# Routed experts of the first layer: lots of 256 rows followed by lots of 128 rows

## The reference

```python
logits = relu(xf @ Wr1 + br1) @ Wr2 + br2          # xf: [8192, 128]
tg, ti = top_k(softmax(logits), 2)                 # two experts of eight
tg = softmax(tg / 2)
out = silu(xf @ Ws1 + bs1) @ Ws2 + bs2             # shared expert
for e in range(8):
    h = silu(xf @ We1[e] + be1[e]) @ We2[e] + be2[e]
    out = out + sum(tg * (ti == e), -1)[:, None] * h
```

## Time and profile before

| What | Value |
|---|---|
| median of three runs | 1275.22 us (1275.15 to 1275.36) |
| span of the profiled execution, first to last instruction | 1271.2 us |
| PE busy | 1153.3 us, 91% of the span |
| DVE busy | 905.4 us, 71% |
| POOL busy | 746.5 us, 59% |
| ACT busy | 674.7 us, 53% |
| first row of `slot_rows` in TensorE | 487.7 us |
| first matmul of the lead | 768.4 us |

### The profile page before, as it was taken

How to read it: one execution, slowest core, us unless ns; L and a number is a source line. 1 busy time by engine, 2 the same in 40 slices (tenths; PEclk the granted TensorE clock), 3 DMA queues, 4 the chain that set the end, 5 groups by cost and what they waited for, 6 DMA issues and landing times. The chain is left out here.

```text
span 1271.2 us, 27145 instructions
## 1 busy us (share of the span) xinstructions
PE 1153.3 (91%) x9434; PEld 829.7 (65%) x9434; DVE 905.4 (71%) x2795; ACT 674.7 (53%) x1088; POOL 746.5 (59%) x908
## 2 busy tenths in 40 slices
PE   3954999999999997999999998999869899889994
PEld 2642555555555546999999896777647677667773
DVE  8986888888888854666666663888765478874442
ACT  4931877777777773444444343555432255553341
POOL 3204788888888752555555552433337657737886
PEclk9975999999999998999999999999889999999997
DMA  9904000000000011222222223212337412255543
GB/s 328 349 1 180 23 27 27 25 25 23 28 28 27 25 32 44 69 72 69 67 73 67 67 63 106 67 53 65 116 106 245 140 41 61 87 193 93 76 54 31
DMA packets 96816, 104.04 MB, mean 82 GB/s; under 512 B 12812, under 2 KB 84300, under 8 KB 96588
## 3 DMA queue, kind: packets, MB, share of 16 engines
q1 hardware_dynamic: 75792, 75.10, 19.1%
q0 software_dynamic: 19968, 26.63, 8.9%
q10 hardware_dynamic: 956, 0.98, 0.2%
HBM read 55.52 MB, written 47.15 MB: 81 GB/s over the span
## 5 line engine op out<-in xcount | busy, mean ns | idle before, releaser
L829 ACT ACTIVATE probs<-ps 128x1024 f32<-128x1024 f32 x256 | 255.1, 1025 | 76.7 <-PE ps L739 76.7
L1148 POOL DMA_INDIRECT y<-slot_y,where x144 | 150.9, 1048 | 144.8 <-DVE slot_y L1129 121.3
L1037 POOL DMA_INDIRECT slots<-rowbuf,slots x192 | 194.3, 1012 | 67.4 <-issue 42.5
L1216 ACT ACTIVATE slot_h<-ps,own 128x256 f32<-128x256 f32 x288 | 120.3, 470 | 152.7 <-PE ps L1180 151.0
L1180 PE MATMUL ps<-slot_x,own 128*128 128x256 f32 x576 | 139.6, 386 | 4.2 <-DVE slot_x L1118 3.5
L1192 PEld LDWEIGHTS ps<-own,slot_h 128*128 128x128 f32 x1152 | 139.7, 192 | 4.0 <-ACT slot_h L1216 0.4
L1192 PE MATMUL ps<-own,slot_h 128*128 128x128 f32 x1152 | 140.2, 275 | 0.0
L755 PE MATMUL ps<-probs,vext 128*32 128x256 f32 x2048 | 137.4, 386 | 0.0
L1697 ACT ACTIVATE h<-ps,packs 128x512 f32<-128x512 f32 x128 | 85.5, 685 | 86.0 <-PE ps L1525 83.5
L1525 PE MATMUL ps<-xT,packs 128*128 128x512 f32 x256 | 119.7, 605 | 10.7 <-ACT h L1697 10.7
L1180 PEld LDWEIGHTS ps<-slot_x,own 128*128 128x128 f32 x576 | 104.6, 192 | 20.6 <-DVE slot_x L1118 9.1
(11 more groups left out here) (301 smaller groups left out, 2291.6 us busy)
## 6 DMA issues: line engine op xcount, KB each, us to landing
toeplitz<-conv_kernel SPq DMA_DIRECT2D x16, 1024.0 KB, 7.0
slots<-blank SPq DMA_DIRECT2D x26, 528.0 KB, 7.2
slot_rows<-slots SPq DMA_DIRECT2D x72, 132.0 KB, 2.1
routed<-y SPq DMA_DIRECT2D x32, 256.0 KB, 3.1
packs<-in_experts SPq DMA_DIRECT2D x1, 4624.0 KB, 14.2
packs<-in_experts SPq DMA_DIRECT2D x8, 578.0 KB, 6.7
xT<-slots SPq DMA_DIRECT2D x16, 264.0 KB, 2.7
stream<-in_x SPq DMA_DIRECT2D x8, 512.0 KB, 8.1
```

What stands on the lines that cost most here:

```text
L829: act.activation(probs[:, p % 4, :, :, :].rearrange("p j k t -> p j (k t)"), ps[:, 2 * (p % 2):2 * (p % 2) + 2, :], ACT.Exp, scale=DK ** - ...
L1037: return pool.indirect_dma_start(m["slot_dram"][layer], bass.IndirectOffsetOnAxis(ap=where, axis=0), m["rowbuf"][:, tile, :], None)
L1148: pool.indirect_dma_start(m["y_dram"][layer], bass.IndirectOffsetOnAxis(ap=where[:, j, h:h + 1], axis=0), y[:, j, h, :], None).then_inc(se ...
L1216: ins = act.activation(hidden[:, j % 2, k, :], ps[:, 2 * (j % 2) + k // 2, (k % 2) * LOT:(k % 2) * LOT + LOT], act_func, bias=own[:, j, P_ ...
```

## The change

The slots of the first layer are rounded up to 128 rows for each expert instead of 256. An expert with n groups of 128 rows gets n // 2 full lots and, where n is odd, one half lot. The first `WHOLE` = 60 lots are full; `HALF_LOTS` = 15 half lots follow, in which full lots beyond 60 are done as two halves. That makes 75 steps instead of 72, with 17280 rows instead of 18432. The 60 full lots are four written out and 14 rounds of the loop instead of 17. The 15 half lots are written out behind the loop in every engine, with the same buffers, order and waits. In a half lot each operation on rows has half its columns or half its count: one transpose, eight matmuls of 128 columns, eight instead of sixteen in `make_out`, one scatter. The copy of the expert's weights and the operations of lines 1098 to 1107 stay, one for each lot. `place_two` gets more instructions, all on VectorE, and the DRAM array of slots is one chunk shorter, so that there are 25 fills with blank rows instead of 26. The second layer isn't changed.

```diff
-LOTS = (2 * TOKENS // LOT + E, TOKENS // LOT)
+WHOLE = 2 * TOKENS // LOT - E // 2
+HALF_LOTS = 2 * (2 * TOKENS // LOT - WHOLE) + E - 1
+STEPS = WHOLE + HALF_LOTS
...
-    for i in range(count, count + max(lag for _, lag in steps)):
+    for i in range(count, count + more + max(lag for _, lag in steps)):
         for step, lag in steps:
             if i - lag < count:
                 step(i - lag, (i - lag) % buffers)
+            elif i - lag < count + more:
+                step(i - lag, (i - lag) % buffers, True)
...
-                c.link(ts(tmp, size, 1.0 / LOT, 0.5 - 0.5 / LOT, ALU.mult, ALU.add))
-                c.link(ts(tmp, tmp, 1.5 * 2.0 ** 23, None, ALU.add))
-                c.link(ts(tmp, tmp, -1.5 * 2.0 ** 23, None, ALU.add))
-                c.link(dve.tensor_tensor_scan(end, ones[:, 0:E], tmp, 0.0, ALU.mult, ALU.add))
-                c.link(tt(start, end, tmp, ALU.subtract))
-                c.link(stt(place[:, :, :], start.unsqueeze(1).broadcast_to([P, TILES, E]),
-                           float(LOT), place[:, :, :], ALU.mult, ALU.add))
+                c.link(ts(tmp, size, 1.0 / P, 0.5 - 0.5 / P, ALU.mult, ALU.add))
+                c.link(ts(tmp, tmp, MAGIC, None, ALU.add))
+                c.link(ts(tmp, tmp, -MAGIC, None, ALU.add))
+                c.link(ts(pairs, tmp, 0.5, -0.25, ALU.mult, ALU.add))
+                c.link(ts(pairs, pairs, MAGIC, None, ALU.add))
+                c.link(ts(pairs, pairs, -MAGIC, None, ALU.add))
+                c.did(dve.tensor_tensor_scan(end, ones[:, 0:E], pairs, 0.0, ALU.mult, ALU.add))
+                c.link(stt(odd, pairs, -2.0, tmp, ALU.mult, ALU.add))
+                c.did(tt(start, end, pairs, ALU.subtract))
+                c.did(ts(far, end, end[:, E - 1:E], -float(LOT), ALU.subtract, ALU.mult))
+                c.link(dve.tensor_tensor_scan(odd_end, ones[:, 0:E], odd, 0.0, ALU.mult, ALU.add))
+                c.did(ts(start, start, float(LOT), None, ALU.mult))
+                c.did(ts(pairs, pairs, float(LOT), None, ALU.mult))
+                c.link(tt(odd, odd_end, odd, ALU.subtract))
+                c.did(stt(far, odd, float(P), far, ALU.mult, ALU.add))
+                c.link(tt(z[:, :, :], place[:, :, :], wide_e(pairs), ALU.is_ge))
+                c.did(tt(place[:, :, :], place[:, :, :], wide_e(start), ALU.add))
+                c.link(tt(z[:, :, :], z[:, :, :], wide_e(far), ALU.mult))
+                c.link(tt(place[:, :, :], place[:, :, :], z[:, :, :], ALU.add))
...
+                c.did(stt(odd_end, end[:, E - 1:E].broadcast_to([P, E]), 2.0, odd_end, ALU.mult, ALU.add))
...
+                c.link(tt(passed[:, :, :],
+                          cst[:, C_HALF:C_HALF + HALF_LOTS].unsqueeze(2).broadcast_to([P, HALF_LOTS, E]),
+                          odd_end.unsqueeze(1).broadcast_to([P, HALF_LOTS, E]), ALU.is_ge))
+                c.did(dve.tensor_reduce(v[4][:, 0:HALF_LOTS], passed[:, :, :], AX.X, ALU.add))
+                c.link(ts(v[1][:, 0:HALF_LOTS], late, float(E), -float(E), ALU.is_ge, ALU.mult))
+                c.link(tt(late, late, v[4][:, 0:HALF_LOTS], ALU.add))
+                c.link(tt(late, late, v[1][:, 0:HALF_LOTS], ALU.add))
...
+            for i in range(HALF_LOTS):
+                j = i % UNROLL
+                sp.wait_ge(sem["downed"], WHOLE + i + 1)
+                sp.wait_ge(sem["weight_ready"], WHOLE + i + 1)
+                sp.dma_start(rows[:, j, 0, :], half_slots[:, i, :]).then_inc(sem[f"rows{j}"], 16)
...
-                for h in range(HALVES):
+                for h in range(halves(half)):
                     pool.indirect_dma_start(
```

## The result

| | before | after |
|---|---|---|
| median time, beside each other | 1275.29 us (1275.15 to 1275.84) | 1268.45 us (1266.56 to 1269.58) |
| ratio | | 0.9942 (0.9928 to 0.9956) |
| the same two kernels a second time, median | 1274.56 us (1270.95 to 1278.77) | 1269.23 us (1266.17 to 1273.87) |
| ratio | | 0.9960 (0.9944 to 0.9976) |

The change makes the kernel faster by 5 to 7 us, 0.4 to 0.6%. I had forecast no change, 1274.0 us, in a range from 1269.0, which the first median lies under and the second, 1269.23, just inside.

The account below looks back on a forecast made before the run. The prediction took TensorE to bound the lots, with VectorE not far behind and bounding half lots from below. Its sum was 1275.2 - 4.7 (lots) + 3.7 (first stage) = 1274.2, forecast as 1274.0 us, range 1269 to 1279.5.

Parts of the forecast that it names:

- First stage, cost 3.7 us (2.4 to 4.5): Start of the kernel: added table work on VectorE delays the first DMA of `attention` by 3.7 us, bounds 2.4 and 4.5.
- my 4.7: First stage: VectorE's added operations for placing and table, less those removed, take 4.7 us more.
- my 0.9: End of the first stage: 0.9 us of VectorE's added work is hidden, since the barrier waits for the table's last store.
- I count from the turn of lot 60 ..., after which the two kernels part: Lots: the kernels differ only from 714.95 us on; 53.5 us to the lead before the change, earlier full lots unchanged.
- TensorE their bound: Full lots: TensorE, busy 272.4 of 276.9 us, sets their pace at some 3.7 us a lot; VectorE needs 3.0.
- Half lots, 2.6 us a step, saving 4.7 us: Last 15 lots: a step between VectorE's 2.5 and the scatter's 2.76 us; lead after 46.7 instead of 51.4 us.
- The pause: Near lot 60: a wait of 2.79 us at 716.08, 2.1 too long, left in both kernels as a full lot's scatter.
- the rival that it goes: Near lot 60: the long wait isn't repeated, 2.1 us go, 1271.9 us; chance 0.30 together with the lower bounds.
- TensorE at 1.9: Rival for the half lots: TensorE bounds them at 1.9 us a step, 1266.3 us in all; chance 0.05.
- a clock that falls throughout the half lots: Rival: idle TensorE drops to 1.2 GHz in the half lots, 3.8 us a step, 1287 us in all; chance 0.03.
- The stage's end and the last stage, taken as unchanged: Behind the lead: no term in the sum, so time from there to the kernel's end was taken to stay the same.
- The surroundings, 4.0 us: Around the profiled span: 4.0 us between the span of 1271.2 us and the median of 1275.22, left as they are.

## Why the prediction was wrong

- *First stage, cost 3.7 us (2.4 to 4.5).* Right: 3.3 us in the pair; on average over six traces each 103.01 with the added operations against 99.67 without. VectorE's surplus is 4.3 for my 4.7, and 1.0 for my 0.9 is hidden under the stores.
- *"I count from the turn of lot 60 ..., after which the two kernels part".* Failed. The full lots ahead of it are 1.6 us shorter from the first copy to that of lot 60 (231.1 and 231.7 us before, 229.4 and 230.4 after; on average 1.6 between the nine traces with 19 more VectorE instructions and the four without), by the loop's rounds of 15.2 us. This term stood at nothing in my sum. I had called TensorE their bound; one lot in four waits for GpSimd in each round, so a tenth on VectorE behind that wait counts.
- *Half lots, 2.6 us a step, saving 4.7 us.* The mechanism was right, the size off: 2.74 us, VectorE's 2.52 with the round trip added in some steps. From turn 60 to lead 53.5 us became 50.4; 4.7 less 11 times 0.14 is 3.2, and 3.1 is what was saved (4.1 in the second pair, with steps of 2.67). The pause is in both kernels, as I had left it; the rival that it goes is dead. TensorE at 1.9 and a clock that falls throughout the half lots are dead too (1.00 from 726 on); a 0.96 over the whole stretch is a fall behind the pause alone.
- *The stage's end and the last stage, taken as unchanged.* Failed, and with the full lots it is the larger part of what the sum missed. I moved the lead and never asked which engine the barrier behind it waits for. It was GpSimd, with four scatters and a drain behind the lead; the half lots leave it two. Gain 1.56 us there, 1.33 of which came back with two scatters, and 0.7 us in the load of `routed` rows, whose cause is open. TensorE's pause of 3.3 us, which I had named for its clock, shrank to 1.7, and its first group with it by 1.5 us; that is hidden under the load.
- *The surroundings, 4.0 us.* A short execution beside others' times; it cancels in a difference.

The sum as measured: +3.3 - 1.6 - 3.1 - 1.6 - 0.7 = -3.7 us, and -4.7 with the lots of the second pair, against -5.3 us in the second pair of medians (-3.1 to -7.1 by the interval of its ratio) and -6.8 in the first. The rest, 0.6 to 3 us, is open: executions of one kernel differ by more, and the last stage alone by 5.7 us between traces; no run here ties that to the change.

## What to carry to other kernels

When a change shortens the tail of a stage, list what each engine still has to do behind the last common step, drain included, and ask which one holds the barrier: the gain may lie there and not in the loop. Then ask what the next stage's first work waits for: TensorE's clock fell behind a long pause here, and these slower matmuls cost nothing, because VectorE waited for a load meanwhile. And where gains of 0.1 us a round count, dead instructions ahead of a loop are a control that belongs beside every edit.

## What the runs showed of the hardware

GpSimd's drain at the barrier behind the lots took 2.26 to 2.99 us, though it began only when its last scatters had landed; ScalarE's took 0.72. A scatter that began while VectorE copied an expert's weights took 0.83 us plus the rest of the copy, and one that began first 0.96. A VectorE loop ran 15.19, 15.26 or 15.36 us a round with 19, 8 or no instructions more ahead of it. The scatter with a pause of 1.9 us ahead of it was the 242nd in all fourteen traces, at times from 714.8 to 718.5 us; its cause wasn't tried. And 27 executions of one kernel on one chip spread over 7.8 us at granted clocks of 0.956 to 0.963.
